# A graph layer on Trainium2: the first tile turned beside the weights, deeper buffers for rows and queries, and edges scattered in batches of 625

## What is computed

```python
xn = layernorm(x)                       # [3125, 1024]
# graph attention, 4 heads of 256
xp = (xn @ W).reshape(N, 4, 256)
e = leaky_relu((xp*att_src).sum(-1)[src] + (xp*att_dst).sum(-1)[dst], 0.2)   # edges and own loops
alpha = softmax of e over the edges of one dst
gnn = relu(segment_sum(xp[src] * alpha, dst) + bias)
# linear attention, 16 heads of 64
Q, K, V = elu(xn @ Wq.T + bq) + 1, elu(xn @ Wk.T + bk) + 1, xn @ Wv.T + bv
out = (Q @ (K.T @ V)) / (Q @ K.sum(0) + 1e-6)
mix = out @ Wo.T + bo
x = x + gnn + mix
x = x + ffn(layernorm(x))               # 1024 -> 512 -> 1024, piecewise linear GELU, fixed point
```

## Time and profile before

| | us |
|---|---|
| three runs | 3398.15, 3409.23, 3412.22 |
| median | 3409.23 |
| the profiled execution, its own time | 3408.76 |
| its span | 3407.0 |
| TensorE busy | 3180.3 (93%) |
| VectorE busy | 2704.7 (79%) |
| ScalarE busy | 1187.2 (35%) |
| GpSimd busy | 1008.2 (30%) |

### The profile page before, as it was taken

The page is one execution under the profiler, slowest core; times in us unless marked ns, Lnnn a source line. Parts: engine busy times, 40 slices in busy tenths (PEclk is TensorE's granted clock), DMA queues, the critical chain, the costliest instruction groups (busy, mean ns, idle before and its releaser), DMA issues. The chain is left out here.

```text
span 3407.0 us, 43255 instructions
## 1 busy us (share of the span) xinstructions
PE 3180.3 (93%) x14812; PEld 2593.8 (76%) x14812; DVE 2704.7 (79%) x4736; ACT 1187.2 (35%) x1521; POOL 1008.2 (30%) x698
## 2 busy tenths in 40 slices
PE   6899999987999999898879999999999996899998
PEld 5678888866888887676668888887888885777776
DVE  5577776756777777457899999999999875888886
ACT  2011111121111111113265565565566443455444
POOL 1247767657766776640000000000000000000000
PEclk8999999998999999999999999999999998999999
DMA  7933323344444445435554453453454223222221
GB/s 253 373 84 71 56 55 72 55 124 79 89 86 90 90 85 128 89 88 152 149 139 122 119 148 86 124 156 99 115 149 117 68 54 105 73 78 72 80 82 43
DMA packets 286025, 366.08 MB, mean 107 GB/s; under 512 B 190330, under 2 KB 190430, under 8 KB 285910
## 3 DMA queue, kind: packets, MB, share of 16 engines
q1 hardware_dynamic: 95828, 282.24, 28.1%
q0 software_dynamic: 184656, 65.68, 11.0%
q10 hardware_dynamic: 5426, 16.70, 1.4%
HBM read 272.64 MB, written 90.80 MB: 107 GB/s over the span
## 5 line engine op out<-in xcount | busy, mean ns | idle before, releaser
L1421 PE MATMUL G_acc<-values,whole_plain 125*125 125x257 f32 x5000 | 1104.9, 383 | 47.6 <-DVE whole_plain L1381 30.0
L1421 PEld LDWEIGHTS G_acc<-values,whole_plain 125*125 125x125 f32 x5000 | 937.7, 189 | 204.6 <-DVE whole_plain L1381 39.7
L331 POOL DMA_INDIRECT counts<-E_twins_now,E_cells_now x400 | 868.4, 2171 | 388.0 <-issue 256.1
L1285 ACT ACTIVATE whole_plain<-whole_plain,G_asrc_slope 125x750 f32<-125x750 f32 (+1 forms) x400 | 377.8, 946 | 418.0 <-DVE whole_plain L1368 417.3
L1368 DVE SCALAR_TENSOR_TENSOR whole_plain<-whole_plain,G_asrc_most 125x750 f32<-125x750 f32 (+1 forms) x400 | 411.3, 1028 | 45.3 <-PE G_acc L1421 44.9
L952 DVE SCALAR_TENSOR_TENSOR N_least<-xT_plain,asrc_all,N_least 125x750 f32<-125x750 bf16 (+1 forms) x336 | 339.1, 1014 | 0.0
L1259 POOL DMA_DIRECT2D gat<-xT_plain x100 | 53.4, 535 | 955.9 <-ACT xT_plain L1301 955.9
L228 PE MATMUL V_v_ps<-whole,xT_space 128*125 128x512 f32 x1200 | 293.2, 402 | 34.7 <-DVE xT_space L256 23.2
L228 PEld LDWEIGHTS V_v_ps<-whole,xT_space 128*125 128x125 f32 x1200 | 221.6, 188 | 106.0 <-DVE xT_space L256 42.1
L228 PE MATMUL Q_q_ps<-whole,xT_space 128*125 128x512 f32 x1200 | 288.0, 399 | 14.0 <-DVE xT_space L256 14.0
L228 PE MATMUL K_v_ps<-K_wv,xT_space 128*125 128x512 f32 x1200 | 293.4, 401 | 0.0
(11 more groups left out here) (183 smaller groups left out, 3517.0 us busy)
## 6 DMA issues: line engine op xcount, KB each, us to landing
whole_plain<-counts SPq DMA_DIRECT2D x222, 328.1 KB
counts<-K_zeros POOLq DMA_DIRECT2D x50, 763.5 KB, 8.6
xT_whole<-xnT SPq DMA_DIRECT2D x75, 500.0 KB
whole_plain<-counts SPq DMA_DIRECT2D x74, 382.8 KB
xnT<-xT_whole SPq DMA_DIRECT2D x25, 500.0 KB
gat<-xT_plain POOLq DMA_DIRECT2D x100, 125.0 KB, 2.3
E_row<-edge_keys ACTq DMA_DIRECT2D x25, 488.3 KB
E_row<-edge_keys SPq DMA_DIRECT2D x25, 488.3 KB
```

The costliest lines, as they stand in the source:

```text
L331: nc.gpsimd.indirect_dma_start(out=counts_cells, out_offset=bass.IndirectOffsetOnAxis(ap=self.cells_now[:, slot, c:c + 1], axis=0), in_=se ...
L1285: nc.scalar.activation(here, here, ACT.Exp, bias=asrc_slope[:, u % H, j:j + 1]).then_inc(exp_ready, 1)
L1421: m = nc.tensor.matmul(acc[0:T, t, 0:CW], weight[:, k % RING, t * T:(t + 1) * T], values[:, j, u % H, :], start=(j == 0), stop=(j == NT - 1))
```

## The change

1. A batch is 5 columns (625 keys), a unit 10 columns (1250 keys), so there are 40 units. How much GpSimd scatters in each block is now counted in batches: 32 in K, 2 in P, 38 in Q and 8 in V. The mask of the comparison is BF16.
2. `SKIP = 5`: in K, tiles 0 to 4 have no unit; units 0 to 19 are prepared in tiles 5 to 24, units 20 to 39 in tiles 0 to 19 of Q. The keys of a unit are loaded after the unit before, in K by ScalarE and in Q by SyncE, as before.
3. The first tile of x is turned in the first block, after the first four pieces of the weights; its high and low part are made there. The edge keys are stored once the first pieces are issued rather than at the block's end. The bias rows `bk`, `bv` are loaded at the start of K, `bq`, `bo` at the start of Q, and VectorE waits for both before its tiles.
4. Rows of x have two places in K; the load runs two tiles ahead.
5. Queries have two places (`q_ps`); TensorE turns query g, computes query g+2 and then mixes tile g. The turned tiles are loaded one further ahead.
6. In V a second place (`xT_other`) takes every other turned tile, loaded two ahead.

The diff, cut to its core:

```diff
-BATCH = 4
+BATCH = 5
 CPU = 2 * BATCH
 UNITS = NCH // CPU
-UNITS_K, UNITS_P, UNITS_Q = 20, 2, 23
+BATCHES_K, BATCHES_P, BATCHES_Q = 32, 2, 38
+SKIP = 5
...
-        self.mask = sb("mask", [CH, 2 * BATCH - 1, CH])
+        self.mask = sb("mask", [CH, 2 * BATCH - 1, CH], BF16)
...
-        for c in range(CPU):
-            if c and c % BATCH == 0:
-                pool.wait_ge(self.scattered, u * (16 * CPU) + 16 * c)
-                pool.sem_inc(self.seen, 1)
+        self.scatter_batch(pool, counts_cells, u, slot, 0)
+
+    def scatter_batch(self, pool, counts_cells, u, slot, batch):
+        nc = self.nc
+        if batch:
+            pool.wait_ge(self.scattered, u * (16 * CPU) + 16 * BATCH)
+            pool.sem_inc(self.seen, 1)
+        for c in range(batch * BATCH, (batch + 1) * BATCH):
...
+        if first % 2:
+            self.scatter_batch(pool, counts_cells, first // 2, first // 2 % 2, 1)
+        unit = (first + 1) // 2
+        if unit == 0:
             self.scatter_unit(pool, counts_cells, 0, 0)
-            first = 1
+            self.scatter_batch(pool, counts_cells, 0, 0, 1)
...
...
-    rows = sb("rows", [T, D])
+    rows = sb("rows", [T, 2, D])
...
+    EARLY = 4
+
+    def take(act, g, slot):
+
+        act.wait_ge(turned, g + 1)
+        nc.scalar.activation(xT_whole[:, :, :], tr[:, :, 0:T], ACT.Copy).then_inc(xT_copied, 1)
+        act.wait_ge(xT_copied, g + 1)
+        high(nc, xT[:, slot, 0, :, :], xT_whole[:, :, :]).then_inc(xT_high, 1)
...
-                load_rows(sp, rows, a["x"][0:T, :], x_loaded)
-                weights.load(sp, blocks)
-                sp.wait_ge(weights.turned, len(blocks))
-                for tile, row in ((bk_row, a["bk"]), (bv_row, a["bv"])):
-                    sp.dma_start(tile[:, :], row.partition_broadcast(T)).then_inc(rows_loaded, 16)
+                load_rows(sp, rows[:, 0, :], a["x"][0:T, :], x_loaded[0])
+                weights.load(sp, range(weights.ring))
                 sp.wait_ge(keys_made, 1)
                 sp.dma_start(a["keys_dram"].rearrange("(b c p) -> c b p", b=CB, p=CH), key_c[:, :, :]).then_inc(keys_stored, 16)
-                sp.wait_ge(rows_loaded, 32)
+                weights.load(sp, range(weights.ring, len(blocks)))
+                load_rows(sp, rows[:, 1, :], rows_of(a["x"], 1), x_loaded[1])
                 sp.wait_ge(keys_stored, 16)
...
-                weights.take_high(act, blocks)
+                weights.take_high(act, range(EARLY))
+                take(act, 0, 0)
+                weights.take_high(act, range(EARLY, len(blocks)))
...
-                weights.take_low(dve, blocks)
+                weights.take_low(dve, range(EARLY))
+                dve.wait_ge(xT_high, 1)
+                low(nc, xT[:, 0, 1, :, :], xT_whole[:, :, :], xT[:, 0, 0, :, :]).then_inc(xT_low, 1)
+                weights.take_low(dve, range(EARLY, len(blocks)))
...
-                weights.turn(pe, blocks)
+                weights.turn(pe, range(EARLY))
+                pe.wait_ge(xn_ready, 1)
+                turn_rows(nc, tr, rows[:, 0, :], ident, turned)
+                weights.turn(pe, range(EARLY, len(blocks)))
...
+            for tile, row in ((bk_row, a["bk"]), (bv_row, a["bv"])):
+                sp.dma_start(tile[:, :], row.partition_broadcast(T)).then_inc(rows_loaded, 16)
+
             def body(g, n):
-                if fixed(g, 0, NT - 2):
+                if fixed(g, 0, NT - 3):
                     sp.wait_ge(turned, g + 1)
-                    load_rows(sp, rows, rows_of(a["x"], g + 1), x_loaded)
+                    load_rows(sp, rows[:, n % 2, :], rows_of(a["x"], g + 2), x_loaded[n % 2])
                 sp.wait_ge(xT_copied, g + 1)
                 sp.dma_start(rows_of(a["xnT_dram"], g, 128), xT_whole[:, :, :].rearrange("p k t -> p (k t)")).then_inc(xT_stored, 16)
-            over_tiles(sp, body)
+            over_tiles(sp, body, tail=3)
...
-                    take(g + 1, (n + 1) % 2)
-                    act.wait_ge(edges.cells_ready, g + 1)
-                    edges.load(act, a["keys_dram"], g + 1)
-            over_tiles(act, body)
+                    take(act, g + 1, (n + 1) % 2)
+                if fixed(g, SKIP):
+                    act.wait_ge(edges.cells_ready, g - (SKIP - 1))
+                    edges.load(act, a["keys_dram"], g - (SKIP - 1))
+            over_tiles(act, body, lead=SKIP + 1)
 
         @block.vector
         def _(dve):
             nc.vector.memset(ones[:, :, :], 1.0).then_inc(ones_set, 1)
             chain = Chain(dve, link)
             chain.step(nc.vector.memset(root[:, :], 0.0))
-            dve.wait_ge(xT_high, 1)
-            low(nc, xT[:, 0, 1, :, :], xT_whole[:, :, :], xT[:, 0, 0, :, :]).then_inc(xT_low, 1)
-            edges.prepare(dve, chain, 0)
+            dve.wait_ge(rows_loaded, 32)
             ahead_of_tiles(chain)
 
             def body(g, n):
                 more = fixed(g, 0, NT - 2)
                 if more:
-                    dve.wait_ge(x_loaded, g * 32 + 64)
-                    normalise(nc, chain, rows[:, :], rows[:, :], stats, moments, root, stats_seen).then_inc(xn_ready, 1)
+                    nxt_rows = rows[:, (n + 1) % 2, :]
+                    dve.wait_ge(x_loaded[(n + 1) % 2], g * 16 + (32 + n % 2 * 16))
+                    normalise(nc, chain, nxt_rows, nxt_rows, stats, moments, root, stats_seen).then_inc(xn_ready, 1)
                 dve.wait_ge(k_done, g + 1)
...
-                if more:
-                    edges.prepare(dve, chain, g + 1)
+                if fixed(g, SKIP):
+                    edges.prepare(dve, chain, g - SKIP)
...
-                sp.wait_ge(weights.turned, 2 * KB)
-                for tile, row in ((bq_row, a["bq"]), (bo_row, a["bo"])):
-                    sp.dma_start(tile[:, :], row.partition_broadcast(T)).then_inc(rows_loaded, 16)
-                sp.wait_ge(rows_loaded, 32)
...
-    q_ps, mix_ps = ps("q_ps", [128, D]), ps("mix_ps", [128, D])
+    q_ps, mix_ps = ps("q_ps", [128, 2, D]), ps("mix_ps", [128, D])
...
+    TWO = dict(lead=2, step=2, tail=SKIP)
...
-            edges.load(sp, a["keys_dram"], NT)
+            for tile, row in ((bq_row, a["bq"]), (bo_row, a["bo"])):
+                sp.dma_start(tile[:, :], row.partition_broadcast(T)).then_inc(rows_loaded, 16)
             load_rows(sp, xin, a["x"][0:T, :], xin_loaded)
-            sp.wait_ge(xT_low, 1)
-            load_turned(sp, 1)
+            for g in (1, 2):
+                sp.wait_ge(xT_low, g)
+                load_turned(sp, g)
 
             def body(g, n):
-                if fixed(g, 0, NT - 3):
-                    sp.wait_ge(xT_low, g + 2)
-                    load_turned(sp, g + 2)
-                elif g == NT - 2:
+                if fixed(g, 0, NT - 4):
+                    sp.wait_ge(xT_low, g + 3)
+                    load_turned(sp, g + 3)
+                elif g == NT - 3:
                     sp.wait_ge(xT_low, NT)
                     load_turned(sp, 0)
-                if fixed(g, 0, NT - 2):
-                    sp.wait_ge(edges.cells_ready, g + 1 + NT)
-                    edges.load(sp, a["keys_dram"], g + (NT + 1))
+                if fixed(g, 0, NT - SKIP - 2):
+                    sp.wait_ge(edges.cells_ready, g + (NT - SKIP + 1))
+                    edges.load(sp, a["keys_dram"], g + (NT - SKIP + 1))
                 if fixed(g, 1):
...
+            act.wait_ge(q_done, 1)
+            act.wait_ge(xn_loaded, 32)
+            high(nc, xT[:, 0, :, :], xT_whole[:, :, :]).then_inc(xT_high, 1)
 
             def body(g, n):
-                if fixed(g, 0, NT - 2):
-                    act.wait_ge(q_done, g + 1)
-                    act.wait_ge(xn_loaded, g * 16 + 32)
-                    high(nc, xT[:, 0, :, :], xT_whole[:, :, :]).then_inc(xT_high, 1)
                 act.wait_ge(q_low, g + 1)
                 nc.scalar.activation(ex[:, :], ex[:, :], ACT.Exp).then_inc(q_exp, 1)
...
-            edges.prepare(dve, chain, NT)
-            ahead_of_tiles(chain)
+            dve.wait_ge(xT_high, 2)
+            low(nc, xT[:, 1, :, :], xT_whole[:, :, :], xT[:, 0, :, :]).then_inc(xT_low, 1)
+            dve.wait_ge(rows_loaded, 32)
...
-                if fixed(g, 0, NT - 2):
-                    dve.wait_ge(xT_high, g + 2)
-                    low(nc, xT[:, 1, :, :], xT_whole[:, :, :], xT[:, 0, :, :]).then_inc(xT_low, 1)
...
+                if fixed(g, 0, NT - 3):
+                    dve.wait_ge(xT_high, g + 3)
+                    low(nc, xT[:, 1, :, :], xT_whole[:, :, :], xT[:, 0, :, :]).then_inc(xT_low, 1)
                 if fixed(g, 1):
                     finish(g - 1)
                 dve.wait_ge(qT_high, g + 1)
                 low(nc, qT[:, 1, :, :], trq[:, :, 0:T], qT[:, 0, :, :]).then_inc(qT_low, 1)
-                if fixed(g, 0, NT - 2):
-                    edges.prepare(dve, chain, g + (NT + 1))
-            over_tiles(dve, body, chain=chain, steps=4 + Edges.STEPS, **ONE)
+                if fixed(g, 0, NT - SKIP - 1):
```

(28 more changed lines are left out.)

84 lines of the change are left out of this document (42 added, 42 removed).

## The result

The changed kernel takes 3437.61 us in the median of four runs (3434.30 to 3447.22), the kernel before 3407.97: a ratio of 1.0096, 95% interval 1.0065 to 1.0127. It is slower by 1%, where I had forecast it 0.8% faster. The profiled execution has a span of 3445.0 us against 3407.0; it is the slowest of the four.

What follows compares the result with a forecast made beforehand. TensorE's time plus holes was taken as the bound, so only holes could close. Terms -11.9 (K), -8.9 (P), -3.7 and -3.8 (Q's entry, exit), +5 (Q's loop), -5 (V) sum to -28: 3381 us, range 3356 to 3404.

Steps and rivals of the forecast that it cites:

- rounds of Q of 25 us: Sign of being wrong: Q's rounds reach 25 us, where 23.1 to 23.6 were expected.
- units of GpSimd that are not 30 us: Sign of being wrong: GpSimd's time for a ten-column unit differs from 30 us.
- Slower than before: Rival in Q: SyncE's loop with keys at half the rate, 9.4 us instead of 4.7; +90, 3466 us; chance 0.07.
- First block: Before K: bias rows and keys no longer hold the block's end; tile 0 starts at 45.4 instead of 58.29, -12.9 us.
- Tile 0's new wait: Start of K: VectorE waits 26 us for bias rows, delaying TensorE's turning of tile 1; +14.1 us, tile 1 at 87.6.
- Tiles 1 to 5: K: no edge work, so nothing waits for the keys; 126.9 us instead of 152.1, -25.2 us.
- GpSimd ends K: K: sixteen GpSimd units of 30.3 us (28.5 to 31.5) end the stage; P starts at 709.6, only -11.9 us.
- P: Second weights: bias rows no longer hold the end, GpSimd has 10 columns, not 16; 43.7 us instead of 52.6, -8.9.
- Q's loop: Q: SyncE's keys, base store and x take 23.3 to 24 us against rounds of 23.14; +5 us (0 to 45).
- the rivals with 25 and with 90 us: Q: SyncE's loop 1.5 us a round longer (25, 3401 us, chance 0.15); keys at half rate (90, 3466 us, chance 0.07).
- Entry and exit of Q: Q: new query order gives 590.6 us instead of 594.3, -3.7; GpSimd no longer last at the exit, -3.8.
- V: Graph values: a second place lets loads of turned tiles run ahead, cutting TensorE's waits; -5 us (0 to -10).

Runs made afterwards that it cites:

- the repaired kernel with batches of 500: Changed kernel with split keys, keys behind x in Q and split, later-awaited bias rows, but batches of four columns, a unit in every tile of K and Q: 3364.43 us.
- the keys behind x: Changed kernel with SyncE's queue in Q reordered: store of base and load of x first, then keys of the next unit: 3381.06 us, ratio 0.9918.
- the fastest one: Changed kernel with split keys, keys behind x in Q, split and later-awaited bias rows, and K's units prepared one tile earlier, 32, 2, 38 batches: 3333.84 us.
- 31, 3 and 38 batches: Changed kernel with split keys, keys behind x in Q, and these batch counts in K, P and Q instead of 32, 2, 38: 3355.90 us, ratio 0.9851.

## Why the prediction was wrong

It named two signs of being wrong, rounds of Q of 25 us and units of GpSimd that are not 30 us, and both came: 26.2 and 32.2. The failed terms are GpSimd's end of K and the loop of Q. "Slower than before" had a chance of 0.07, for a longer loop of Q alone; for K no rival had a slower GpSimd. By its own steps:

- **First block** (-12.9): right, even better: 42.49 instead of 45.4, -15.8. I had added 2 us for the turned first tile and put the block's end at 44.8; VectorE was done with its part at 41.6, earlier than before (42.8).
- **Tile 0's new wait** (+14.1): right in kind, a little large: tile 1 at 82.76, 40.3 us after tile 0, where I had 42.2. VectorE got the bias rows at 66.68, 24.2 us after TensorE's start; I had 26.
- **Tiles 1 to 5** (-25.2): right: 25.3 us each from 82.76 on. But the reason given, no edge work, is one of several: with fast loads the kernel before gained 19 of the 25 us with its edge work, and the repaired kernel with batches of 500 has units in these tiles and takes 25.4 us for each.
- **GpSimd ends K** (units of 30.3, 28.5 to 31.5): right mechanism, failed size, and outside its bounds: 32.2. The failed term is the fence. I took its length from the kernel before, 2.97 us in the mean, as a constant. It depended on where in the unit a load of keys fell, and 25.3 us a unit beside 25.37 us a tile had held that place fixed. With 32.2 beside 25.3 every place comes up, and a third of the fences meets a load. 31 fences with 1 us more are the 30 us (-11.9 forecast, +13.2 measured; the first unit came 5 us early). What TensorE alone would allow was mis-stated too: I left out VectorE's unit in the last tile, about 7 us, hidden here under GpSimd.
- **P** (-8.9): 48.9 us from its start to the first query (734.7 to 783.62) against 54.9: -6.0. TensorE begins it at half its clock after 45 us of idle time (the first product takes 3.78 us). That doesn't explain the 2.9 us that it lasted longer than forecast: with the keys behind x its first product took 3.78 us as well, behind a wait of 34.91, and it lasted 46.4. What does explain it stays open. Two windows (columns as above), of the changed kernel and of the fastest one, where that wait is 2 us:

```profile
735.00:739.00 4.00, 4.00 (x7) 1.74 (x8) 1.53 (x3) 0.00 (x0) 2.80 (x3) 0.50 0.72 257
```

```profile
679.50:682.00 2.50, 1.98 (x4) 0.66 (x4) 1.81 (x3) 0.00 (x0) 1.60 (x2) 1.00 0.74 213
```

- **Q's loop** (+5, 0 to 45): the failed step, with GpSimd's. The mechanism was named: SyncE issues the keys when the unit is done, and only then stores base. The unit was done 12.4 us after the start of finish, as written; but from the issue of the keys to that of x it took 9.5 us, where I had 7.8, and x another 4.1 where I had 3.0 to 3.4. I had taken rows of single transfers and added them; run behind each other and beside GpSimd's they took 13.6 where the sum said about 11. The term of the store was the worst: I had let it end 1.3 us behind the keys, but from 1086.8 to 1091.8 the engines still moved 83 to 117 GB/s. An excess of 3.0 us a round, 17 times, gives 51: outside the term's bounds, and between the rivals with 25 and with 90 us. With 0.8 us of slack in a loop of five steps, an error of some 25% in two of them was the whole loss in Q.
- **Entry and exit of Q** (-7.5): with rounds of 23.2 us (the keys behind x) the first query to the last mix takes 595.5 us against 594.3 before, so the new order of queries gave nothing, where I had -3.7; the exit gave 4.6 (10.7 to 6.1).
- **V** (-5, 0 to -10): -21, and all of it the second place. I had held VectorE's 5.7 us a product for the next bound, but it is busy for only 212.7 of the 305.4 us. Of the 20.6 us between the two windows of V 9.0 are TensorE's busy time, with the same instructions; how much of that is the clock (0.97 and 0.98) and how much are gaps too short to be told from work stays open.

Sum: K to P's start +13 in place of -12, Q's loop +51 in place of +5, V -21 in place of -5, the others within 3 us each but for Q's entry (+1 in place of -4); these make the 34.8 us by which G starts later. The range failed since both misses have one root, the load of keys to 125 partitions, and I had set their bounds apart: the rule on what stands behind such a load stood in my text as a remark on Q and V, and no term for K had it. The rest of the change is sound: with the keys loaded in two parts in both kernels it is 39 us faster (3354.11 against 3393.39), where I had 28. That doesn't bear out the sum either, since V gave 21 and not 5.

## What to carry to other kernels

A wait measured in a periodic kernel holds only for its phase: when an edit changes the period of one engine against another, take the fence at its worst place too, not at its mean. A load to 125 partitions is worth cutting into 112 and 13: the same bytes, and here neither its own queue nor the fences of GpSimd were held up as before. Other numbers of partitions were not run. A loop that goes through a DMA queue is to be added up with every transfer at its contended duration, and a transfer that nobody is waiting for (here the keys) belongs behind those that somebody is waiting for.

## What the runs showed of the hardware

- A DMA of 610 KB to 125 partitions lengthened the landing of small indirect DMAs of another queue from about 3 to 5.6 us in the mean, and up to 7.8; with a store right behind it to 8.8. As 112 and 13 partitions it left them at 2.9. Two loads of 500 KB each to 125 partitions made one of 10.1 in the kernel before with the split keys.
- That DMA moved 133 GB/s with 0.33 of the DMA engines' time. In two parts, from 1.0 to 3.0 us behind its issue, the engines moved 283 GB/s with 1.01 of their time, and 21 GB/s in the next 3 us.
- In the kernel before, loading the same keys in two parts took 22.7 us out of K, though the DMA engines moved 382 GB/s between 81 and 96 us, as before (383): from the issue of the second load of keys to VectorE's first use of it, it took 11.4 us (76.61 to 88.03) instead of 16.1 (80.08 to 96.16).
- After 45 us of idle time TensorE's granted clock was 0.50, the lower of its two levels (1.2 GHz), for the first products, and so it was after 9.33 us (31, 3 and 38 batches); after 2.06 us it was 1.00 (the unit one tile earlier). But short waits were not free either: in a round of Q of the changed kernel TensorE waited 2.38 us for the scaled query, and behind the turning the clock was 0.50 from 1067 to 1070, so that the query took 12.99 us:

```profile
1065.82 1.07 PE L244 MATMUL Q_trq<-ident,Q_q 125*128 125x125 f32 x8 [2.38 <-DVE Q_q L859]
1066.93 12.99 PE L229 MATMUL Q_q_ps<-whole,xT_space 128*125 128x512 f32 x48
```

In the next round, behind a wait of 0.79 us, it took 11.45. The round was not longer for it, since VectorE waited for x.
